# Counting edges by (node within 32, quarter of sources), and a fused VectorE selector per step

## The reference, cut to what matters

```python
# layers 0 and 1: messages with a weight and a relation per edge, summed at dst
coef = comp[etypes]
m = sum(coef[:, b, None] * (h @ basis[b])[src] for b in bases) * norm[:, None]
agg = segment_sum(m, dst)
# layer 2: in-degree and mean over incoming edges
deg = maximum(segment_sum(ones(E), dst), 1.0)
agg = segment_sum(feat[src], dst);  ah = agg / deg[:, None]
out = feat @ W1 + b1 + ah @ W2 + b2
# layer 3: attention only along edges; an edge that occurs twice counts twice
scores = einsum('ehd,ehd->eh', q[src], k[dst]);  smax = segment_max(scores, src)
ex = exp(scores - smax[src]);  attn = ex / segment_sum(ex, src)[src]
out = segment_sum(attn[:, :, None] * v[dst], src)
```

## Time and profile before

| stage | us from the start | length |
|---|---|---|
| tables | 0 to 42.7 | 42.7 |
| L0a: first aggregation and counting | 42.7 to 349.7 | 307.0 |
| G turned | 349.7 to 370.0 | 20.3 |
| first transform, counts stored | 370.0 to 535.0 | 165.0 |
| L0b: second aggregation, G not yet turned | 535.0 to 766.0 | 231.0 |
| L0b: last steps with turning | 766.0 to 806.0 | 40.0 |
| second transform | 806.0 to 938.0 | 132.0 |
| L1: third aggregation, G not yet turned | 938.0 to 1130.0 | 192.0 |
| L1: last steps with turning | 1130.0 to 1232.0 | 102.0 |
| third transform | 1232.0 to 1469.0 | 237.0 |
| layer 2 up to the turned counts | 1469.0 to 1566.0 | 97.0 |
| rest of layer 2, layer 3 | 1566.0 to 3179.2 | 1613.2 |

### The profile page before, as it was taken

The page is one execution under the profiler, slowest core; times in us unless marked ns, Lnnn a source line. Parts: engine busy times, 40 slices in busy tenths (PEclk is TensorE's granted clock), DMA queues, the critical chain, the costliest instruction groups (busy, mean ns, idle before and its releaser), DMA issues.

```text
span 3179.2 us, 44609 instructions
## 1 busy us (share of the span) xinstructions
PE 3042.3 (96%) x14954; PEld 2194.2 (69%) x14954; DVE 2097.8 (66%) x4794; ACT 1382.1 (43%) x2130; POOL 1161.1 (37%) x938
## 2 busy tenths in 40 slices
PE   7999998999979999999999999999999999999999
PEld 3334676444753346876448998789988899879987
DVE  7999423787348864254367678667776777767777
ACT  7999632001340023342254555345543555435554
POOL 4555336556356643431204022511125111441023
PEclk9999998999989999999999999999999999999999
DMA  3555433556236643324103011220014001130012
GB/s 95 149 145 149 165 103 113 162 164 176 79 103 176 170 138 101 97 68 143 33 30 106 8 37 50 66 70 14 31 50 125 18 8 64 43 103 14 8 64 79
DMA packets 125748, 279.37 MB, mean 88 GB/s; under 512 B 22727, under 2 KB 40455, under 8 KB 124499
## 3 DMA queue, kind: packets, MB, share of 16 engines
q0 software_dynamic: 40320, 132.15, 14.8%
q1 hardware_dynamic: 83762, 141.72, 14.2%
q10 hardware_dynamic: 1440, 2.62, 0.2%
HBM read 227.83 MB, written 27.46 MB: 80 GB/s over the span
## 4 chain that ended last, share of the span: by engine, by line
PE 79%; DVE 12%; issue 3%; DMA 3%; ACT 2%; POOL 1%; DVEq 0%; SPq 0%; POOLq 0%; ACTq 0%
PE bank L152 15%; PE bank L154 15%; PE bank L153 15%; PE bank L864 13%; PE bank L2465 5%; PE bank L875 4%; DVE G L988 4%; PE bank L2129 3%; PE bank L1771 2%; PE bank L839 2%; DVE y_tile L2081 1%; DVE y_tile L2083 1%; DVE x_stats L2064 1%; PE bank L1047 1%; DMA yT_lo<-yT_new_lo 1%
## 5 line engine op out<-in xcount | busy, mean ns | idle before, releaser
L864 PE MATMUL bank<-gathered,selector 128*128 x1328 | 659.7, 612 | 52.5 <-SPq L827 30.2
L988 DVE TENSOR_TENSOR G<-G,bank 128x512 f32 x664 | 454.8, 685 | 154.3 <-PE bank L864 102.3
L864 PEld LDWEIGHTS bank<-gathered,selector 128*128 128x128 f32 x1328 | 219.2, 191 | 326.3 <-issue 301.4
L2553 ACT CAST probT<-bank 128x512 fp32r<-128x512 f32 (+2 forms) x480 | 212.1, 516 | 263.8 <-PE bank L2465 262.9
L2635 DVE CUSTOM_DVE_ANT_0 prob<-bank,count_by_src 128x512 f32<-128x512 f32 (+1 forms) x480 | 258.3, 588 | 60.4 <-PE bank L154 60.4
L849 ACT COPY G<-bank 128x512 f32<-128x512 f32 x160 | 81.2, 658 | 497.7 <-PE bank L839 497.7
L1445 POOL TENSOR_TENSOR weight_parts<-weight_ring,weight_parts 128x512 fp32r<-128x512 f32 x130 | 187.3, 1441 | 301.0 <-ACT weight_parts L1378 300.9
L891 ACT ACTIVATE sign_src<-node_iota_16bit,src_float 128x1251 bf16<-128x1251 f16 x208 | 278.6, 1341 | 41.6 <-PE bank L875 19.3
L1404 DVE TENSOR_TENSOR lhs_parts<-G,lhs_parts 128x640 fp32r<-128x640 f32 x122 | 101.5, 832 | 293.9 <-ACT lhs_parts L1376 293.7
L2561 DVE TENSOR_TENSOR probT<-bank,probT 128x512 fp32r<-128x512 f32 (+2 forms) x480 | 254.2, 585 | 51.0 <-ACT probT L2553 50.2
L152 PE MATMUL bank<-weight_parts,lhs_parts 128*128 128x512 f32 x680 | 268.0, 394 | 9.4 <-POOL weight_parts L1445 4.5
(11 more groups left out here) (293 smaller groups left out, 6935.2 us busy)
## 6 DMA issues: line engine op xcount, KB each, us to landing
weight_ring<-in_L_gnn_basis SPq DMA_DIRECT2D x64, 256.0 KB, 2.8
weight_ring<-in_L_gnn_bases SPq DMA_DIRECT2D x64, 256.0 KB, 2.7
x_L<-x_rows SPq DMA_DIRECT2D x50, 256.0 KB, 4.4
x_rows<-x_L SPq DMA_DIRECT2D x50, 256.0 KB, 5.7
yT_hi<-yT_new_hi SPq DMA_DIRECT2D x4, 2560.0 KB, 10.8
yT_lo<-yT_new_lo SPq DMA_DIRECT2D x4, 2560.0 KB
count_rows<-count SPq DMA_DIRECT2D x10, 640.0 KB, 5.9
count_by_dst<-count_rows SPq DMA_DIRECT2D x10, 640.0 KB, 8.3
```

The lines of the kernel that those rows point to most:

```text
L864: pe.matmul(bank[s % banks][:], sel[:, s % SELECTORS, :], xs[:, ds(slot[s % BATCH], 1), :].rearrange("p t d -> p (t d)"), start=True, stop ...
L988: dve.tensor_tensor(g, g, bank[s % banks][:], ALU.add).then_inc(*added.inc())
L2553: ins = act.copy(hi, of)
```

## The change

Three things change.

First, the counting. `PATHC` has windows of 32 nodes, 40 of them, and 82 steps of four tiles, so 328 units. A source s is split into its quarter (s // 320) and the rest; the one-hot has 128 places, (node within 32) times (quarter of the source), and the signs have 321 columns. One product of 321 columns does what three did, and one add of 321 columns per four units. The 328 units are spread evenly over the 208 steps of L0a (`units_at`): one or two per step. The banks of L0a become four for G and two for the counts; the signs have a ring of eight. The quarter and the rest are computed on DVE in `prepare`, for 42 x 512 edges.

Second, the selector. In all three aggregations DVE makes the selector of one step in one instruction (compare, then multiply), eight steps ahead, right after an add of G.

Third, what reads the counts. They lie in memory as rows of nodes, four quarters of 321 each. The store writes ten pieces of four windows, in rows of 1284 bytes where it had 5120. `layer_2` reads a ring of four tiles of 1284 columns, writes the differences into tiles of their own, and sums four degrees per node at the end.

```diff
-SIGNS = [(c, min(512, N + 1 - c)) for c in range(0, N + 1, 512)]
+HIGHS = 4
+LOW = NP // HIGHS
+SIGNS = LOW + 1
+COUNT_ROW = HIGHS * SIGNS
-PATH0, PATH1, PATHC = Path(5, 16), Path(4, 4), Path(7, 4, 4)
+PATH0, PATH1, PATHC = Path(5, 16), Path(4, 4), Path(5, 2, 4)
...
-        for n in ("src", "dst"):
-            dve.tensor_copy(grouped[n][0:PATHC.groups], grouped_i[n][0:PATHC.groups]).then_inc(*converted.inc())
+        src, dst, high = (grouped[n][0:PATHC.groups] for n in ("src", "dst", "high"))
+        dve.tensor_copy(src, grouped_i["src"][0:PATHC.groups]).then_inc(*converted.inc())
+        dve.tensor_copy(dst, grouped_i["dst"][0:PATHC.groups]).then_inc(*converted.inc())
+        dve.wait_ge(*converted.now())
+        dve.tensor_scalar(high, src, float(LOW), None, ALU.is_ge).then_inc(*converted.inc())
+        for a in range(2, HIGHS):
+            dve.wait_ge(*converted.now())
+            dve.scalar_tensor_tensor(high, src, float(a * LOW), high, ALU.is_ge, ALU.add).then_inc(*converted.inc())
+        dve.wait_ge(*converted.now())
+        dve.scalar_tensor_tensor(src, high, -float(LOW), src, ALU.mult, ALU.add).then_inc(*converted.inc())
+        dve.scalar_tensor_tensor(dst, dst, float(HIGHS), high, ALU.mult, ALU.add).then_inc(*converted.inc())
...
-SELECTORS = 3 * BATCH
+SELECTORS, AHEAD = 3 * BATCH, 2 * BATCH
+COUNT_BANKS, SIGN_RING = 2, 8
...
-    banks = 2 if counting else 3
+    banks = 4 if counting else 3
...
+    def units_at(s):
+        return range(units * s // steps, units * (s + 1) // steps)
...
             if counting:
-                c, q = divmod(s, PATHC.tiles)
-                if q == 0:
-                    pe.wait_ge(*hot(c + 1))
-                    if c >= 2:
-                        pe.wait_ge(*summed(len(SPANS) * (c - 1)))
-                pe.wait_ge(*signed(s + 1))
-                for m, (col, width) in enumerate(SIGNS):
-                    ins = pe.matmul(bank[2 + 3 * (c % 2) + m][:, 0:width], counting.oh_dst[:, c % 2, q, :],
-                                    counting.sign_src[:, q, col:col + width], start=q == 0, stop=q == PATHC.tiles - 1)
-                ins.then_inc(*counted.inc())
+                for u in units_at(s):
+                    c, q = divmod(u, PATHC.tiles)
+                    if q == 0:
+                        pe.wait_ge(*hot(c + 1))
+                        if c >= COUNT_BANKS:
+                            pe.wait_ge(*summed(c - COUNT_BANKS + 1))
+                    pe.wait_ge(*signed(u + 1))
+                    pe.matmul(bank[banks + c % COUNT_BANKS][:, 0:SIGNS], counting.oh_dst[:, c % 2, q, :],
+                              counting.sign_src[:, u % SIGN_RING, 0:SIGNS], start=q == 0,
+                              stop=q == PATHC.tiles - 1).then_inc(*counted.inc())
...
-    def select(i):
...
+    def select(s):
+        if s >= SELECTORS:
+            dve.wait_ge(*multiplied(s - SELECTORS + 1))
+        dve.scalar_tensor_tensor(
+            sel[:, s % SELECTORS, :].rearrange("p (b n) -> p b n", b=nb),
+            grid.rearrange("p (b n) -> p b n", b=1).to_broadcast([P, nb, path.nodes]), C.place[path][:, s:s + 1],
+            co[:, :, s:s + 1].to_broadcast([P, nb, path.nodes]), ALU.is_equal, ALU.mult).then_inc(*selected.inc())
...
             dve.tensor_tensor(g, g, bank[s % banks][:], ALU.add).then_inc(*added.inc())
+            if s + AHEAD < steps:
+                select(s + AHEAD)
             if counting:
-                c, m = divmod(s, PATHC.tiles)
-                if c and m:
-                    count_add(c - 1, m - 1, count_windows[c - 1])
...
+                for c in range(PATHC.steps):
+                    if last_step[c] == s - 1:
...
+                        count_add(c, count_windows[c])
+                        if c + 2 < PATHC.steps:
+                            count_one_hot(c + 2)
...
-        sp.dma_start(self.C.count_rows[:, j * NP:(j + 1) * NP], self.count[:, j, :]).then_inc(*self.stored.inc())
+        windows = self.C.count_rows.rearrange("n (a b) -> (n a) b", a=HIGHS).rearrange("(w p) b -> p w b", p=P)
+        four = slice(4 * j, 4 * j + 4)
+        sp.dma_start(windows[:, four, :], self.count[:, four, :]).then_inc(*self.stored.inc())
...
-        dve.tensor_tensor(C.rdeg[:, j:j + 1], row[:, 0:1], row[:, N:N + 1], ALU.subtract).then_inc(*degree.inc())
-        dve.wait_ge(*degree.now())
-        dve.tensor_tensor(row[:, 0:N], row[:, 0:N], row[:, 1:N + 1], ALU.subtract).then_inc(*differed.inc())
-        dve.wait_ge(*differed.now())
-        dve.memset(row[:, N:NP], 0.0).then_inc(*differed.inc())
+        dve.tensor_tensor(tops[:, j, :], row[:, :, 0], row[:, :, LOW], ALU.subtract).then_inc(*topped.inc())
...
+        dve.tensor_tensor(differences[:, j % APART, :].rearrange("p (a b) -> p a b", a=HIGHS), row[:, :, 0:LOW],
+                          row[:, :, 1:SIGNS], ALU.subtract).then_inc(*differed.inc())
```

More of the change, by code:

```diff
@@ L766, in aggregate @@
     if counting:
-        grid, same = C.iota[:, 0:path.nodes], M.new("same_node", [P, BATCH, path.nodes])
+        grid = C.iota[:, 0:path.nodes]
     else:
         grid = bank[3][:, 0:path.nodes]
-        same = bank[3][:, P:P + BATCH * path.nodes].rearrange("p (t n) -> p t n", t=BATCH)
     gathered = [C.landed(f"gathered{u}") for u in range(RING)]
@@ L778, in aggregate @@
     turned, taken = C.event("G_turned"), C.event("G_taken")
-    batches = -(-steps // BATCH)
     per = P // path.nodes
@@ L783, in aggregate, with step_of @@
     lag = 4
+    units = PATHC.steps * PATHC.tiles
+    def units_at(s):
+        return range(units * s // steps, units * (s + 1) // steps)
+    def step_of(unit):
+        return next(s for s in range(steps) if unit in units_at(s))
+    first_step = [step_of(c * PATHC.tiles) for c in range(PATHC.steps)]
+    last_step = [step_of((c + 1) * PATHC.tiles - 1) for c in range(PATHC.steps)]
     def turns_after(s):
@@ L903, in on_act @@
             act.wait_ge(*counting.numbered)
-            for s in range(steps):
-                sign(s)
+            for u in range(units):
+                sign(u)
         else:
@@ L946, in count_one_hot, with count_add @@
             ALU.is_equal).then_inc(*hot.inc())
[L948 to L949 removed]
+    def count_add(c, w):
         dve.wait_ge(*counted((c + 1) * PATHC.tiles))
[L951 to L954 removed]
+        if c:
+            dve.wait_ge(*summed(c))
+        to = counting.count[:, ds(w, 1), :].rearrange("p a n -> p (a n)")
+        dve.tensor_tensor(to, to, bank[banks + c % COUNT_BANKS][:, 0:SIGNS], ALU.add).then_inc(*summed.inc())
     def on_dve():
@@ L961, in on_dve @@
             dve.wait_ge(*laid(1))
-        select(0)
-        select(1)
+        for s in range(AHEAD):
+            select(s)
         if counting:
             count_one_hot(0)
-        if counting:
+            count_one_hot(1)
             dve.wait_ge(*counting.cleared)
@@ L1724, in layer_2 @@
     pe, act, dve, pool, sp = C.engines
+    ROWS, APART = 4, 4
     M.at = C.keep2 + 2 * 4 * KC * D
```

110 lines of the change are left out of this document (46 added, 64 removed).

## The result

The changed kernel takes 3173.59 us (median of 5 runs, 3168.56 to 3180.66); before, in the same series, 3198.17 us (5 runs, 3192.58 to 3200.82). The ratio is 0.9924, 95% interval 0.9911 to 0.9936: 24.6 us faster, where I had forecast 62. The profiled execution takes 3168.56 us, its span is 3167.1 us.

What follows compares the result with a forecast made beforehand. PE was taken to bound L0a and most of L0b, DVE's adds L1. Tables +3.7, L0a -38, store +3, L0b -5 and L1 -26 sum to -62 us: 3136 us from 3198.2, range 3108 to 3172.

Steps and rivals of the forecast that it cites:

- L1's: L1 up to its turning: DVE's step falls from 1.04 to 0.89 us, -26 us, leaving 166 us.
- Next in line are PE, 179 x 0.88 = 158 us: L1: after DVE, PE would be the next limit at 158 us, just under the 166 us that remain.
- my first rival: L0b and L1: something else takes DVE's place, L1 gives half, L0b nothing; 3154 us, chance 0.12.
- L0a: First aggregation: fewer count instructions, DVE becomes the limit at about 269 us instead of 307.0, -38 us.
- Tables: Table stage: five more 512-element DVE instructions, each waiting for the one before, +3.7 us.
- Store: Store of the counts: rows of 1284 instead of 5120 bytes slow the DMA, all on the path, +3 us.
- second rival: Store of the counts: it swallows a third of the gain, +24 us instead of +3; 3157 us, chance 0.09.
- L0b: Aggregation L0b: the same 14% saving on DVE's 16% of the chain, -5 us.
- Layer 2: Layer 2: differences in two instructions instead of three, but DVE waits for PE there, 0 us.
- a step of 1.15: Aggregations: the previous add's report takes effect only after the selector, so steps lengthen; 3247 us, chance 0.08.
- no overlap: Aggregations: DVE's instructions do not overlap, a step is 1.03 us; 3210 us, chance 0.03.
- wrong if L0a does not fall below 285: Sign in the profile after: the whole forecast is wrong if L0a stays at 285 us or more.

Runs made afterwards that it cites:

- z1: y1 with DVE adding only 8 of the 512 columns of each product into G in L0b and L1: 3180.71 us, ratio to before 0.9923.
- y1: The changed kernel with one register operation (and with 1023) on each table value that PE and POOL wait against: 3176.53 us, ratio to before 0.9937.
- y4: y1 with a one-column copy on DVE between the add and the selector of every step of L0b and L1: 3181.13 us, ratio to before 0.9949.
- y2: The kernel before with the same register operation on the table values as y1: 3201.21 us, ratio to before 1.0008.
- g3: y1 with the selectors of before (two instructions for four steps) in L0b and L1: 3184.34 us, ratio to before 0.9957.
- x1: The changed kernel with the two tables that PE and POOL read taken as 16-bit halves: 3239.12 us, ratio to before 1.0110.
- y3: y1 with gathers of 1 KB rows instead of 2 KB in L0b and L1, each product reading its half twice: 3172.14 us, ratio to before 0.9933.

## Why the prediction was wrong

**The step that failed is L1's**, in its second half: "Next in line are PE, 179 x 0.88 = 158 us". The first half held: DVE's step is 0.90. The 0.88 us came from L0a's chain, as a product's share of it (183.9 us over 208 steps), where count products stood between. In L1's rows products do start 0.86 us apart for a dozen steps, but that is not what PE delivers over the stage. The earlier trace rows held a warning that the prediction passed over: PE was busy 174.2 us in L1, more than the 166 that it left the stage (a warning and not a bound, since the ends of PE's records are modelled). The column "mean" of the table is the finding: with DVE at 0.86, 0.90, 0.96 or 1.04 us, with whole or half gathers, three banks or four, pauses or none, L1's steps come out at 1.02 to 1.07 us on average. Where the pace between gaps is quicker, gaps fill it up: 32.1 us of them at 0.86 (z1), 21.8 at 0.90 (y1), 11.7 at 0.96 (y4), 4.6 or less at 1.04 (y2, g3). With PE slowed to 1.13 (x1) there is nothing left to fill. The kernel before ran DVE at 1.04, just at that pace, so DVE ended the waits in its chain and PE's limit was not to be seen. This is the mechanism of my first rival; it gave L1 half of the gain, and the runs leave it 1 to 4 us of 26. Against y2, y1 gained 23 us of the 62 forecast; of the 39 that are missing, 22.5 are L1's up to its turning and 15.6 L0a's.

That PE's side sets 1.03 is shown: its products, its table loads or its signals. Which of them is not. The runs exclude VectorE, the gathers' bytes, the wait for selectors at each step, the grid in PSUM and the number of banks; the trace of after excludes the landing of tiles. The clock that the trace shows was granted in full (1.00, the upper of TensorE's two levels, 2.4 GHz) from 973 us on to the end of L1, while gaps went on. What remains is PE itself, or the way its signals leave it. One rival stands untested: two table loads of 0.33 us in four steps are 0.16 us a step, about what lies between 0.86 and 1.03, and no run left them out. Against it: in z1, 126 of 180 products start 0.86 us after the one before, at all four places of a batch of four steps, so in close stretches the loads cost nothing. A hint is open as well: of the signals of L1's 181 products the trace holds 181 in the first profile of before and 111 in that of after, so that recording itself may be part of it. But y2 holds only 129 and g3 126, with one gap and two. The Trainium skill, "NOTIFIC — the notification-queue block", section "7.1 Overflow: three behaviours, one of which stalls the engine", has a setting in which a full queue of records holds its engine up; no run here shows whether that happens.

**L0a** was to fall by 38 and fell by 25 (22 against y2). DVE's terms of the sum were right: 126 spacings of 0.895 and 81 of 1.87, where a count stands between, make 264 us, against 264.6 forecast. The rest of the 278.7 us, 14.5 us, is the waiting in DVE's first line above: 5 us in one stretch about 70 us from the start, where DVE, ACT and POOL stood idle at once (3.28, 4.97 and 2.76 us; ACT's wait was for PE), and some 10 scattered. It looks like the lateness of L1, which no run isolated here; I had allowed "some stalls" without a price.

**Tables** +3.7: measured +3.5 to +4.9. **Store** +3: the last piece took 11.61 us instead of 7.93, but against y2 the whole way from L0a to L0b is +0.6 (+6.2 in the two first profiles): no second rival. **L0b** -5: -2.7. **Layer 2** 0: +0.1 with all that follows. The two slower rivals, a step of 1.15 and no overlap, are excluded by the 0.90.

My sign "wrong if L0a does not fall below 285" did not fire: it watched the stage that was sure, not the one on which 26 us hung.

## What to carry to other kernels

- A second limit "just under" the first is a rival of its own. Its price has to be read from a stretch as long as the stage in which that engine is the bound, not from its share of another stage's chain or from its quickest rows: 0.88 us a product by the share, 0.86 in short stretches, 1.03 over L1.
- Before speeding up an engine, make its work nearly nothing in a copy of the kernel (adds of 8 columns here). If the stage doesn't move, the gain was never there; here one such run (z1) said so.
- An execution that is 17 us quicker than its median has its difference somewhere; here it was largely in the stages under study, and differences of a few us between single profiles of L0b or L1 mean nothing.

## What was not expected of the hardware

- In the gap shown, PE's signals came up to 2.5 us late and in a clump (968.21, 968.29, 968.33) while its rows showed products of 0.43 us a pass in close order.
- A load of four table values into registers took 0.33 us, or 0.93 to 0.98 us when only every second 16-bit value was read (y1, x1).
- Gathers of half the bytes took POOL as long to issue (0.96 us each, y3) and did not shorten L1.
